# Keys loaded as four paced transfers of 32 partitions, and pooled rows moved at the middle of a step

## The reference

```python
feat = concatenate([qe, k, qe - k, qe * k], axis=-1)      # 4 * 128 features
h = feat @ W1 + b1                                        # 64 hidden
h = where(h >= 0, h, alpha * h)
a = (h @ W2 + b2)[..., 0]
a = where(mask == 0, -1e9, a)
w = softmax(a, axis=-1)
y = einsum('bl,bld->bd', w, k)                            # 2048 x 128
```

## Time and profile before

| | |
|---|---|
| median of three runs | 1115.57 us (1104.18 to 1120.39) |
| profiled execution | 1110.33 us, span 1108.6 us |
| mean granted TensorE clock | 0.96 |
| busy share of the span | PE 76%, PEld 55%, DVE 69%, ACT 47%, POOL 59% |
| DMA | 222.42 MB, mean 201 GB/s |
| keys transfers | 128, 1600.0 KB each, 7.7 us from issue to landing (median) |

### The profile page before, as it was taken

How to read it: one execution, slowest core, us unless ns; L and a number is a source line. 1 busy time by engine, 2 the same in 40 slices (tenths; PEclk the granted TensorE clock), 3 DMA queues, 4 the chain that set the end, 5 groups by cost and what they waited for, 6 DMA issues and landing times.

```text
span 1108.6 us, 55080 instructions
## 1 busy us (share of the span) xinstructions
PE 839.3 (76%) x25216; PEld 609.9 (55%) x25216; DVE 765.0 (69%) x1143; ACT 517.3 (47%) x1281; POOL 652.5 (59%) x401
## 2 busy tenths in 40 slices
PE   0568777777788877777787777778877877878776
PEld 0345555555566655555565555555655555555555
DVE  3788777676677766766678676676777667667671
ACT  0355455444455544544455444445555435545452
POOL 1766666655566665645576655656656655557551
PEclk9999999999999999988899999999999989889999
DMA  8906556656556654654556655556656646456420
GB/s 272 382 14 243 189 208 229 237 174 209 189 200 236 248 198 176 246 190 178 181 209 239 236 184 203 185 189 219 220 192 241 233 147 241 158 215 231 171 104 11
DMA packets 48583, 222.42 MB, mean 201 GB/s; under 512 B 23264, under 2 KB 31456, under 8 KB 31968
## 3 DMA queue, kind: packets, MB, share of 16 engines
q1 hardware_dynamic: 48352, 218.91, 55.1%
HBM read 214.57 MB, written 4.33 MB: 197 GB/s over the span
## 4 chain that ended last, share of the span: by engine, by line
PE 50%; ACT 17%; DVE 16%; issue 15%; SPq 1%; DMA 1%; POOL 0%; DVEq 0%; ACTq 0%; POOLq 0%
PE hP L409 39%; ACT act L262 16%; DVE act L317 10%; PE poolP L433 8%; DVE keysT L312 3%; PE scoreP L421 2%; PE poolP L441 1%; DMA w2c<-in_L_rec_W 1%; DVE logits L324 1%; ACT pooled L298 1%; DVE neg_max L330 1%; PE hP L452 0%; DVE qX L350 0%; SPq L146 0%; DVE bias L363 0%
## 5 line engine op out<-in xcount | busy, mean ns | idle before, releaser
L262 ACT ACTIVATE act<-hP,biast,al 128x200 f32<-128x200 f32 x1024 | 446.3, 516 | 440.1 <-PE hP L409 440.0
L409 PE MATMUL hP<-keysT,weff 32*64 32x200 f32 x16384 | 455.6, 343 | 150.9 <-DVE act L317 91.8
L312 DVE STREAM_TRANSPOSE keysT<-keys 128x768 f32<-128x768 f32 (+1 forms) x512 | 509.8, 996 | 0.0
L317 DVE TENSOR_TENSOR act<-hP,act 128x400 f32<-128x400 f32 x512 | 283.9, 554 | 303.8 <-ACT act L262 303.7
L409 PEld LDWEIGHTS hP<-keysT,weff 32*64 32x64 f32 x16384 | 338.5, 134 | 240.0 <-issue 136.6
L213 POOL TENSOR_TENSOR weff<-weff_q,wk 128x1024 f32<-128x1024 f32 x128 | 302.4, 2363 | 285.5 <-PE hP L409 284.0
L433 PE MATMUL poolP<-keys,pool_w 128*16 128x128 f32 x6400 | 252.1, 284 | 64.2 <-ACT pooled L298 49.9
L433 PEld LDWEIGHTS poolP<-keys,pool_w 128*16 128x16 f32 x6400 | 200.5, 100 | 106.8 <-issue 81.5
L208 POOL TENSOR_TENSOR weff_q<-qX,wp 128x1024 f32<-128x1024 f32 x128 | 243.7, 1904 | 24.1 <-DVE qX L350 23.7
L248 POOL TENSOR_TENSOR pool_w<-probs_k,own_b 128x400 f32<-128x400 f32 x128 | 110.9, 867 | 135.5 <-PE poolP L433 74.8
L421 PE MATMUL scoreP<-act,w2win 128*16 128x200 f32 x2048 | 144.0, 346 | 20.1 <-DVE act L317 10.1
(11 more groups left out here) (35 smaller groups left out, 28.6 us busy)
## 6 DMA issues: line engine op xcount, KB each, us to landing
keys<-in_r_k SPq DMA_DIRECT2D x128, 1600.0 KB, 7.7
probs_scratch<-expd SPq DMA_DIRECT2D x32, 100.0 KB, 2.6
masks<-in_r_mask SPq DMA_DIRECT2D x128, 12.5 KB
probs_k<-probs_scratch SPq DMA_DIRECT2D x128, 12.5 KB
out_rows<-pooled SPq DMA_DIRECT2D x128, 8.0 KB
keys<-in_r_q SPq DMA_DIRECT2D x4, 256.0 KB, 5.0
w<-in_L_rec_W SPq DMA_DIRECT2D x4, 128.0 KB, 6.6
b1c<-in_L_rec_b SPq DMA_DIRECT2D x2, 0.2 KB, 8.8
```

The source lines that it names most:

```text
L262: a_.activation(act[:, k, a, :], hP[:, BANK[k][a], 0:L], ACT.Identity, bias=biast[:, n, k, a:a + 1], scale=al[:]).then_inc(t_done, 1)
L312: v_.transpose(keysT[:, n % 2, j0 * D:j1 * D], keys[:, n % SLOTS, j0 * D:j1 * D]).then_inc(keysT_done, 1)
L317: v_.tensor_tensor(act[:, k, 2 * pair:2 * pair + 2, :], hP[:, bank:bank + 2, 0:L], act[:, k, 2 * pair:2 * pair + 2, :], ALU.max).then_inc( ...
L409: mm = t_.matmul(hP[H * r:H * r + H, BANK[k][a], 0:L], weff[QP * a:QP * a + QP, n % 2, w, c, :], kT[QP * a:QP * a + QP, :, c, KP * w:KP * ...
```

## The change

A tile of keys is no longer one transfer of 128 partitions but four of 32, one per quadrant, each 409,600 bytes; all four count on the tile's `keys_in`, which VectorE now awaits at 64. In the main loop, quad a of tile n+3 waits until VectorE has done 4(n+1)+2+a pieces: quad 0 for piece 1 of tile n+1 (and, as before, for the slot), quad 1 for piece 2 of it, quad 2 for piece 3, quad 3 for piece 0 of tile n+2. SyncE issues quad 0 ahead of the masks, quads 1 and 2 behind them, and quad 3 behind the exchange of the exponentials through HBM. In the prologue the load of tile n waits for tile n-2 from tile 3 on. ScalarE's move of the pooled rows stands ahead of scale_half(n, 1), no longer behind it.

```diff
--- before.py
+++ after.py
@@ -29,6 +29,7 @@
 CD = D // QP
 HALVES = 2
 CUTS = [0, 6, 12, 18, J]
+PIECES = len(CUTS) - 1
 HEAD_J = 12
 BANK = [[0, 1, 2, 3], [0, 1, 4, 5]]
 NEG = -1000000000.0
@@ -40,7 +41,7 @@
 
 
 def attention_pooling(nc, r_q, r_k, r_mask, W1, b1, alpha, W2, b2, out):
-    k_tiles = r_k.rearrange("(n b) (i j) d -> n (b i) (j d)", b=SUB, i=KP)
+    k_quads = r_k.rearrange("(n a b) (i j) d -> n a (b i) (j d)", a=QUADS, b=BQ, i=KP)
     mask_rows = r_mask.rearrange("(g s c w) l -> g c s w l", s=GT, c=QUADS, w=BQ)
     out_rows = out.rearrange("(g s c w) d -> g c s w d", s=GT, c=QUADS, w=BQ)
     q_rows = r_q.rearrange("(t y a w) d -> a y t (w d)", y=QP, a=QUADS, w=BQ)
@@ -142,8 +143,12 @@
 
         @block.sync
         def _(sp):
+            def load_quad(n, a):
+                sp.dma_start(keys[QP * a:QP * a + QP, n % SLOTS, :], k_quads[n, a]).then_inc(keys_in[n % SLOTS], 16)
+
             def load_keys(n):
-                sp.dma_start(keys[:, n % SLOTS, :], k_tiles[n]).then_inc(keys_in[n % SLOTS], 16)
+                for a in range(QUADS):
+                    load_quad(n, a)
 
             def load_mask(g):
                 for c in range(QUADS):
@@ -163,6 +168,8 @@
                 sp.dma_start(b1c[H * r:H * r + H, :], b1.rearrange("(a b) -> a b", b=1)).then_inc(params_in, 16)
                 sp.dma_start(w2c[H * r:H * r + H, :], W2).then_inc(params_in, 16)
             for n in range(1, SLOTS):
+                if n > 2:
+                    sp.wait_ge(keys_in[n - 2], 16 * QUADS)
                 if n == 3:
                     sp.wait_ge(zeroed, 1)
                     load_mask(0)
@@ -172,14 +179,22 @@
                 load_keys(n)
 
             for n in range(STEPS):
+
+                def paced_quad(a):
+                    if SLOTS <= n + AHEAD < TILES:
+                        ge(sp, keysT_done, min(PIECES * (n + 1) + 2 + a, PIECES * TILES))
+                        load_quad(n + AHEAD, a)
+
                 if SLOTS <= n + AHEAD < TILES:
 
                     sp.wait_ge(part_done, n + AHEAD - SLOTS + 1)
-                    load_keys(n + AHEAD)
+                paced_quad(0)
                 g = n // GT - 1
                 if n % GT == 1 and 0 <= g < GROUPS - 2:
                     sp.wait_ge(scores_read, g + 1)
                     load_mask(g + 2)
+                paced_quad(1)
+                paced_quad(2)
                 if n % GT == 0 and 0 <= g < GROUPS:
                     sp.wait_ge(exp_done, g + 1)
 
@@ -189,6 +204,7 @@
                     for t in range(GT):
                         sp.dma_start(probs_k[:, g % 2, t, :], probs_tiles[g % 2, t]
                                      ).then_inc(probs_in[GT * (g % 2) + t], 16)
+                paced_quad(3)
                 m = n - 1 - LAG
                 if m % GT == GT - 1 and 0 <= m < TILES:
                     g = m // GT
@@ -288,15 +304,16 @@
                     if g + 1 < GROUPS:
                         act_e.wait_ge(exp_done, g + 1)
                         fill(g + 1)
-                if n < TILES:
-                    scale_half(n, 1)
                 if m % GT == GT - 1 and 0 <= m < TILES:
+
                     g = m // GT
                     act_e.wait_ge(pooled_done, g + 1)
                     act_e.wait_ge(inv_done, g + 1)
                     ge(act_e, out_done[g % 2], g // 2 * 16 * QUADS)
                     a_.activation(pooled[:, g % 2, :], poolP[:, D:2 * D], ACT.Copy,
                                   scale=inv_sum[:, g % 2:g % 2 + 1]).then_inc(pooled_moved, 1)
+                if n < TILES:
+                    scale_half(n, 1)
 
         @block.vector
         def _(dve):
@@ -306,7 +323,7 @@
                 if n >= TILES:
                     return
                 if piece == 0:
-                    dve.wait_ge(keys_in[n % SLOTS], (n // SLOTS + 1) * 16)
+                    dve.wait_ge(keys_in[n % SLOTS], (n // SLOTS + 1) * 16 * QUADS)
                     ge(dve, main_done, HALVES * (n - 1))
                 j0, j1 = CUTS[piece:piece + 2]
                 v_.transpose(keysT[:, n % 2, j0 * D:j1 * D], keys[:, n % SLOTS, j0 * D:j1 * D]).then_inc(keysT_done, 1)
@@ -397,7 +414,7 @@
 
             def first_layer(n, k):
                 if k == 0:
-                    pe.wait_ge(keysT_done, (len(CUTS) - 1) * (n + 1))
+                    pe.wait_ge(keysT_done, PIECES * (n + 1))
                     pe.wait_ge(weff_done, n + 1)
 
                 ge(pe, act_done, 2 * (HALVES * n + k) - 1)
```

## The result

The changed kernel took 1289.22 us (median of four, 1285.17 to 1291.97) against 1115.59 us: ratio 1.161, 95% interval 1.155 to 1.167. Slower was forecast, by 6%, with 1225 us as the range's upper end; it is 16% slower. The profiled execution has a span of 1289.9 us and a mean granted clock of 0.876.

What follows compares the result with a forecast made beforehand. The DMA engines were to become the bound: tile 0 in at 20.5 us, 127 tiles x 7.8 = 990.6, 30 exchanges x 4.3 = 129, then 6.2, 28.7 and 1.7, together 1177 us. The 8-in-10 range was 1000 to 1225 us.

Steps and rivals of the forecast that it cites:

- Rate of 32 partitions: Keys transfers: four of 32 partitions go at q's 210 GB/s, 7.8 us a tile instead of 4.0.
- the two readings of q: Load of q at the start: its 210 GB/s comes from its 32 partitions or from its short 2 KB runs.
- The DMA engines as the bound: Main loop: transfers need 7.8 us a tile against the engines' 6.8, so VectorE waits at piece 0 of every tile.
- The hole behind the exchange: Once a group, quad 3 waits behind the softmax exchange and no keys move for 4.3 us; 129 us in 30.
- The pacing costs nothing by itself: Quads' waits for transposes: quad 3 follows 1 us after the landing, with two quads (3.9 us) still ahead; no cost.
- The prologue "nothing": Load of the first tiles: the new waits leave two tiles in flight, so they cost nothing.
- an earlier first tile: Start of the sum: tile 0, which landed at 16.7 us, needs 3.8 us more and is in at 20.5 us.
- Pooled rows: ScalarE's earlier move: TensorE's 49.9 us of waits in late steps go; a late step falls from 8.8 to about 7.1 us.
- Rival 1: Keys transfers: quads run at full rate, 1 us each; floor 928 us, about 1010 us in all; chance 0.22.
- the fourth quad's delay: In the full-rate case, quad 3 lands 9.1 us after piece 3, wanted at 7.4; 1.7 us in 32 groups, 54 us.
- Rival 3: TensorE's clock stays low, a step takes 8.0 us: 1215 to 1230 us; sign, mean clock below some 0.75; chance 0.08.
- The rule of the Trainium skill on the DMA engines' turns between queues: Each DMA engine goes round its queues packet by packet, so instructions would not be held back for a whole tile.

Runs made afterwards that it cites:

- spread_paced: The changed kernel, but each of the four transfers takes every fourth partition instead of 32 adjacent ones, with the same waits: 1094.71 us, ratio 0.986.
- late reads: The changed kernel with the wait for the exponentials' write and its four reads moved into the next step behind quad 0, masks a step later: 1183.55 us.
- tiny_keys: The kernel before with pooled rows moved early and main-loop keys transfers cut to 16 of 3200 columns: 928.45 us, ratio 0.832.
- unpaced quads: The changed kernel with all four quads issued together as soon as the slot is free, ahead of everything else in the step: 1393.77 us, ratio 1.252.
- with columns: The changed kernel, but each transfer is all 128 partitions by a quarter of the columns: 1062.53 us unpaced, 1002.11 us paced with the late reads.
- quads_wait_less: The changed kernel with all four waits for transposes two pieces earlier, the queue's order kept: 1292.31 us, ratio 1.159.

## Why the prediction was right and wrong

- **Rate of 32 partitions: right.** 7.8 us a tile was forecast from q's 210 GB/s; it is 8.0 us in a full queue (127 x 0.2 = 25 us more) and 7.6 us in the prologue. Of the two readings of q that I had left open, the changed kernel's own 12.8 KB runs rule out the short runs, and the spread quads show that it is the adjacent partitions. The rule of the Trainium skill (SBUF — State Buffer, "Door 1: The DMA port swizzle") stands: 217 GB/s in the window above where it says 218, and 64 adjacent partitions no better than 32.
- **The DMA engines as the bound: right once in a group, wrong as stated.** The share of the DMA queue went from 55.1% of 1108.6 us to 76.0% of 1289.9 us, where above 90% was forecast, and VectorE was to wait at every tile. It waits in 46 of them, 130 us, at the exchange and just behind it. In the other two tiles of a group the keys are in before VectorE wants them, though the queue is as full.
- **The hole behind the exchange: right.** 4.3 us forecast, 4.5 measured, 134 us in all (129 forecast). The late reads took 106 us back. Moving quad 3 alone took back 50, since most of the hole moved to the next tile.
- **"The pacing costs nothing by itself", with TensorE's standstills left out of the sum: this step failed.** I had counted standstills as a loss of the kernel before only. With slow keys they got longer: ahead of all TensorE's work 134 us (103.0 + 23.6 + 7.7) after, 77 us before. Its matmuls took 934.9 us where they had taken 839.3, in part at the lower clock. Two rows of the changed kernel in order of time, in a step behind an output, show a standstill and what it does to VectorE, whose transposes then release quads late:

```profile
605.77 0.95 PE L426 MATMUL hP<-keysT,weff 32*64 32x200 f32 x11 [3.22 <-issue]
...
607.76 0.57 DVE L334 TENSOR_TENSOR act<-hP,act 128x400 f32<-128x400 f32 x1 [4.10 <-ACT act L278]
```

  So the queue, nearly always full otherwise, runs empty ahead of quads other than 3 (38 us from tile 11 on), and starts slowly after each hole; together 2.2 us a group beyond my terms, 64 us. In the 13 of 29 groups with at most 0.4 us of such empty queue a group takes 37.3 us, in the other 16 it takes 40.1 us (forecast 35.5). That the longer groups are the standstills' doing is argued, not isolated: over the 29 groups, the time and the standstills in it go together only loosely (correlation 0.48). What the runs show is that without the main loop's bytes, where 8 us of standstills are left, order and waits cost some 7 us (23 less the prologue's 16), and that lifting the waits by two pieces gains nothing, while standstills ahead of the first layer grow to 165 us.
- **The prologue "nothing": failed, 16 us.** Tile 10's first packet comes 24 us after tile 9's, not 8. SyncE's queue in order of time:

```profile
80.31 0.35 SPq L202 DMA_DIRECT2D probs_scratch<-expd  x1
89.04 2.25 SPq L205 DMA_DIRECT2D probs_k<-probs_scratch  x4
91.33 2.72 SPq L155 DMA_DIRECT2D masks<-in_r_mask  x4
102.21 11.15 SPq L147 DMA_DIRECT2D keys<-in_r_k  x7
```

  Tile 10 waits for the pooling of tile 0, and the first nine steps took 78 us instead of 63. It is not the new waits: spread_paced has them too, and its nine steps take 63 us at a clock of 1.00. Beside keys at half the rate the clock is 0.75 in the window above, and nine halves of steps 1 to 5 take 2.9 to 6.0 us for their 64 first-layer passes instead of 1.61. That is longer than the 2.45 us of the lower clock, so the clock alone isn't it; instructions trickling in behind the keys would fit, and no run isolates it. Before, all ten tiles were in by 56 us and the pause hid behind them; at half the rate the lead is used up, as I had said, and then the pause counts.
- **The sum again:** 1177, and 25 for the tiles, 5 for the exchanges, 64, 16, less 3 for an earlier first tile: 1284 of 1289 us. The 64 us are what the group's measured 38.9 us leave over, so that the sum closes does not confirm their cause.
- **Pooled rows: right as a mechanism, 50 us forecast, 37 by itself,** nothing in the changed kernel.
- **Rival 1** had the right kernel in mind and the wrong partitions. Its floor, 928 us, is tiny_keys' 928.45 us; its time, 1010 us, is that of the spread quads only with the late reads (1014.56), and 1095 without: I had priced the fourth quad's delay at 54 us, and it cost 80. **Rival 3**, the clock, did not decide by its own sign, a mean below 0.75: it was 0.876. Its 1215 to 1230 us did not follow from its terms either; 127 steps of 8.0 us in the forecast's sum make 1202.
- A slip in the working: the change adds 3 issues a tile, 12 a group, not 12 a tile. It does not touch the sum, which had them at nothing.
- The rule of the Trainium skill on the DMA engines' turns between queues (DMA: Bandwidth & Descriptors, "Queues, rings and completion order") is not refuted, as I had taken it to be. A packet there holds some 9 to 17 descriptors; a tile of 128 rows over 16 DMA engines is 8 of the trace's packets on each, and may all be one turn. Standstills ahead of the first layer were 66 us at runs of 3.1 to 3.6 KB and 65 us at 12.8 KB, both unpaced; 24 to 43 us paced, at the full rate; none in tiny_keys. Which DMA engine serves the instructions, and how long they wait for their turn, no run shows.

## What to carry to other kernels

Cut a large load so that every piece still reaches partitions of both halves, by columns or by every fourth partition; a block of 32 or 64 adjacent ones runs at half the rate. Cut and spaced, the pieces gained 88 us here, where a long instruction stream stands behind bulk loads. But then every item in the queue's order counts: no wait for a round trip may stand ahead of a piece. And when a transfer becomes slower, ask what else waits in its queue, and price that too.

## What the runs showed of the hardware that I had not expected

- TensorE's instructions wait behind keys: 77 us of standstills in the kernel before, 304 us with unpaced quads, 2 us in tiny_keys, with the same number of TensorE's matmuls in all of them. Nine in ten of the longer ones end 1.2 to 1.6 us after a 16 KB block of instructions has come in.
- The length of the runs did not matter for it. How much of a tile stood in the queue at one time did: with columns, 95 us unpaced (66.2 + 25.4 + 3.5 + 0.2), 43 us paced with the late reads (35.1 + 4.5 + 3.7).
- The granted clock mostly followed: 0.864 in the kernel with the longest standstills, 0.96 before, 0.992 in tiny_keys. It does not go by their sum alone: 0.890 with 235 us of them in quads_wait_less, 0.876 with 134 us in the changed kernel.
